# Two-layer attention and expert kernel: the last stage's order of work on five engines, the key rows' swap, and the last expert chunks

## The reference

```python
x = x + L0_xattn(layernorm(x), ctx, ctx, ...)    # 16 heads, causal
x = x + L0_ffn(layernorm(x), ...)                # shared + 64 experts, top 8
x = x + L1_xattn(layernorm(x), ctx, ctx, ...)
x = x + L1_ffn(layernorm(x), ...)                # ternary weights
# L1_xattn, for each head:
corr = irfft(rfft(Q) * conj(rfft(K)))            # along the 64 rows
corr_mean = corr.mean(axis=-1)                   # over the head's 8 columns
top_w, top_idx = top_k(corr_mean, 4)             # the "delays"
top_w = softmax(top_w)
out = sum_i(top_w[i] * roll(V, top_idx[i]))
out = out @ Wo + bo
```

## The kernel before

| lag | what | engine before |
|---|---|---|
| 0 | normed input `held` (L1210, `norm_in`) | GpSimd |
| 1 | transform `l_pf` (L1560), copied to `l_xf` (L1498, L1499) | PE, ACT |
| 2 | `l_pq` = query, key and value rows of each of the two tiles (L1548 to L1551), copied to `l_qkv` (L1493), product `l_pp` (L1352) | PE, ACT, POOL |
| 3 | sums over head columns, `l_sums` (L1437) | DVE |
| 9 | values times weights, `l_rr` in two halves (L1315) | half POOL, half DVE |
| 10 | `l_po` (L1537), `l_oT` (L1486), `l_py` (L1571, L1572) | PE, ACT, PE |
| 11 | added to `x_res` (L1412), statistics (L1428, L1445), `l_rstd` (L1344, L1346) | DVE, POOL |
| 12 to 14 | `l_zn` (L1452), turned `l_pt` (L1584), `xnT` (L1508), `amax` (L1458) | DVE, PE, ACT, DVE |

## Time and profile before

### The profile page before, as it was taken

How to read it: one execution, slowest core, us unless ns; L and a number is a source line. 1 busy time by engine, 2 the same in 40 slices (tenths; PEclk the granted TensorE clock), 3 DMA queues, 4 the chain that set the end, 5 groups by cost and what they waited for, 6 DMA issues and landing times. The chain is left out here.

```text
span 1321.7 us, 30877 instructions
## 1 busy us (share of the span) xinstructions
PE 1262.8 (96%) x9258; PEld 1016.0 (77%) x9258; DVE 1061.2 (80%) x2054; ACT 905.8 (69%) x1472; POOL 821.4 (62%) x868
## 2 busy tenths in 40 slices
PE   6999999996999999999999999999999998899986
PEld 4777777775788887887878887888878886799975
DVE  4878888884987988988977987988977985367786
ACT  3778888883777777777777776777667775566640
POOL 3766666652565665755665665755665666799960
PEclk8999999996999999999999999999999999999998
DMA  4410101001987676777687687677687583110004
GB/s 119 113 30 28 32 28 32 28 16 39 207 193 177 162 181 164 178 189 172 156 191 173 153 191 164 172 185 175 159 194 171 154 194 74 33 29 28 18 2 128
DMA packets 126227, 159.64 MB, mean 121 GB/s; under 512 B 20856, under 2 KB 59520, under 8 KB 126144
## 3 DMA queue, kind: packets, MB, share of 16 engines
q1 hardware_dynamic: 125054, 158.29, 49.7%
q10 hardware_dynamic: 1090, 0.43, 0.1%
HBM read 152.25 MB, written 6.42 MB: 120 GB/s over the span
## 5 line engine op out<-in xcount | busy, mean ns | idle before, releaser
L1032 DVE TENSOR_TENSOR e_m<-e_pu,raw 128x1024 f32<-128x1024 f32 x256 | 309.8, 1212 | 87.5 <-ACT e_pu L1089 55.8
L1089 ACT ACTIVATE e_pu<-e_pu 128x1024 f32<-128x1024 f32 x256 | 258.7, 1010 | 148.7 <-PE e_pu L1125 146.3
L1099 ACT CAST e_mh<-e_m 128x1024 fp32r<-128x1024 f32 x256 | 268.3, 1048 | 60.4 <-DVE e_m L1032 59.1
L1037 DVE TENSOR_TENSOR e_ml<-e_m,e_mh 128x1024 fp32r<-128x1024 f32 x176 | 239.4, 1360 | 20.4 <-ACT e_mh L1099 19.4
L951 POOL TENSOR_TENSOR e_ml<-e_m,e_mh 128x1024 fp32r<-128x1024 f32 x80 | 193.2, 2418 | 90.0 <-ACT e_mh L1099 90.0
L1123 PE MATMUL e_pu<-r_xh,wuh 128*128 128x512 f32 x528 | 215.4, 408 | 2.5 <-PEq L208 1.9
L1134 PE MATMUL e_py<-e_mh,wdh 128*128 128x512 f32 x528 | 208.5, 395 | 3.4 <-ACT held L1076 3.4
L1125 PE MATMUL e_pu<-r_xl,wuh 128*128 128x512 f32 x528 | 209.5, 397 | 0.0
L1124 PE MATMUL e_pu<-r_xh,wul 128*128 128x512 f32 x528 | 209.5, 397 | 0.0
L1135 PE MATMUL e_py<-e_mh,wdl 128*128 128x512 f32 x528 | 209.1, 396 | 0.0
L1138 PE MATMUL e_py<-e_ml,wdh 128*128 128x512 f32 x528 | 168.4, 397 | 2.2 <-POOL e_ml L951 1.4
(11 more groups left out here) (232 smaller groups left out, 2499.6 us busy)
## 6 DMA issues: line engine op xcount, KB each, us to landing
raw<-gates_scratch SPq DMA_DIRECT2D x512, 256.0 KB, 4.3
x_res<-in_x_dram SPq DMA_DIRECT2D x64, 64.0 KB, 1.8
xcT<-in_ctxT_dram SPq DMA_DIRECT2D x64, 64.0 KB, 1.9
held<-in_ctx_dram SPq DMA_DIRECT2D x32, 128.0 KB, 2.1
out_dram<-t_res SPq DMA_DIRECT2D x16, 256.0 KB, 2.3
gates_scratch<-raw SPq DMA_DIRECT2D x17, 128.0 KB, 2.3
raw<-in_L_ffn_W_up_dram SPq DMA_DIRECT2D x4, 512.0 KB, 4.5
raw<-in_L_ffn_W_down_dram SPq DMA_DIRECT2D x4, 512.0 KB, 5.5
```

Of the source, the lines that this page charges most:

```text
L1032: nc.vector.tensor_tensor(flat(m[r % 3][:]), flat(pu[r % 3][:]), flat(gt[i % SPREAD]), ALU.mult).then_inc(gated, 1)
L1037: nc.vector.tensor_tensor(flat(ml[k][:]), flat(m[k][:]), flat(mh[k][:]).bitcast(F32), ALU.subtract).then_inc(m_low[0], 1)
L1089: nc.scalar.activation(flat(pu[k][:]), flat(pu[k][:]), ACT.Silu).then_inc(silued, 1)
L1099: nc.scalar.copy(flat(mh[k][:]), flat(m[k][:])).then_inc(m_high, 1)
```

## The change

In **experts**, `drive` loops over four iterations (chunks 1 to 12) and writes chunks 13 to 15 out, so that work for chunks that don't exist can be left out (`exists`). The padding and its memset go. `norm_in` moves from GpSimd to VectorE.

In **tail**, TensorE begins a step with `l_py` of the item whose `l_oT` was made a step earlier (lag 11 instead of 10), then `l_pf`, `l_po`, `l_pt`, and the two `l_pq` last; in group steps L1578 comes before the two `l_pq` and L1590 between them. L1548's product of the shifted copy is gone, and so is the copy L1499; `l_pq` has three parts instead of four, and ScalarE writes the swapped key rows with two copies of 64 partitions each. `norm_in` runs on VectorE instead of GpSimd, both halves of `l_rr` on GpSimd instead of one, and the order of VectorE's step changes. There are 46 steps.

```diff
 # experts: drive
+    looped = (chunks - 4) // 3 * 3
-            with eng.Fori(0, (chunks - 1) // 3) as g:
+            with eng.Fori(0, looped // 3) as g:
...
-            for n in range(turns, turns + RING):
-                step(n, GROUPS + n % GROUPS, lambda lag, n=n: (n - lag) // GROUPS)
+            for n in range((1 + looped) * GROUPS, turns + RING):
+                step(n, n % (3 * GROUPS), lambda lag, n=n: (n - lag) // GROUPS)
+        def exists(c):
+            return not isinstance(c, int) or c < chunks
 # each step: routing of chunk c + 1 under "if exists(c + 1)", norm of c + 2 under "if exists(c + 2)"
-                    if i == 12:
+                    if i == 12 and exists(c + 2):
                         norm(c + 2)
...
 # GpSimd, end of experts
-                for n in range(2):
-                    entry.norm_in(x_res, y_mean, y_rstd, n)
 # VectorE, end of experts
+                dve.wait_ge(y_rooted, 4)
+                for n in range(2):
+                    entry.norm_in(x_res, y_mean, y_rstd, n)
 # tail: ScalarE's copies of the projections
-                            nc.scalar.copy(qkv[:, n % SLOTS, j], pq[j][:]).then_inc(q_out, 1)
+                            nc.scalar.copy(qkv[:, n % SLOTS, j, 1:4, :], pq[j][:])
+                            nc.scalar.copy(qkv[S:, n % SLOTS, j, 0, :], pq[j][0:S, 1, :])
+                            nc.scalar.copy(qkv[0:S, n % SLOTS, j, 0, :], pq[j][S:, 1, :]).then_inc(q_out, 1)
...
-                        nc.scalar.copy(xf[:, n % 2, :, :, 0:P], pf[n % 2][:])
-                        nc.scalar.copy(xf[:, n % 2, :, 1, P:], pf[n % 2][:, :, 1, 0:S]).then_inc(f_out, 1)
+                        nc.scalar.copy(xf[:, n % 2], pf[n % 2][:]).then_inc(f_out, 1)
 # tail: TensorE's projections
-                            nc.tensor.matmul(pq[j][:, 0, :], k_swapped, cst["w1T"][:, 1, :], start=True, stop=False)
-                            nc.tensor.matmul(pq[j][:, 1, :], q, cst["w1T"][:, 0, :], start=False, stop=False)
-                            nc.tensor.matmul(pq[j][:, 2:4, :], k, cst["w1T"][:, 1:3, :], start=False, stop=False)
+                            nc.tensor.matmul(pq[j][:, 0, :], xf[:, n % 2, j, 0, :], cst["w1T"][:, 0, :], start=True, stop=False)
+                            nc.tensor.matmul(pq[j][:, 1:3, :], xf[:, n % 2, j, 1, :], cst["w1T"][:, 1:3, :], start=False, stop=False)
 # tail: GpSimd
-                        gated(nc.gpsimd, n, 0).then_inc(mixed[0], 1)
-                    if on(s, 0) and s >= 2:
...
-                        entry.norm_in(x_res, y_mean, y_rstd, n)
+                        gated(n, 0)
+                        gated(n, 1).then_inc(mixed, 1)
```

More of the change, by code:

```diff
@@ L955, in step @@
                     c, first = chunk(0), isinstance(n, int) and n < GROUPS
[L956 to L969, removed]
-                    if i == 12:
+                    if exists(c + 1):
+                        if i == 1:
+                            routing.low_part(pool, c + 1, (r // GROUPS + 1) % 3)
+                        if i == 2:
+                            routing.ends(pool, nc.gpsimd, "pool", c + 1)
+                        if i == 3:
+                            routing.fourth_powers(pool, nc.gpsimd, "pool", c + 1)
+                        if i == 4:
+                            routing.denominator(pool, nc.gpsimd, "pool", c + 1)
+                        if i == 9:
+                            routing.weights(pool, nc.gpsimd, "pool", c + 1)
+                        if i == 11:
+                            routing.gates_of(pool, nc.gpsimd, "pool", c + 1)
+                    if i == 9 and not first:
+                        y_root(c - 1)
+                    if i == 12 and exists(c + 2):
                         norm(c + 2)
                 drive(pool, step)
-                for n in range(2):
-                    entry.norm_in(x_res, y_mean, y_rstd, n)
             @block.sync
@@ L1041, in step @@
                     c, first = chunk(0), isinstance(n, int) and n < GROUPS
[L1042 to L1048, removed]
-                            y_add(c - 1)
-                    if i == 6:
-                        routing.compare(dve, c + 1)
-                        routing.invert(dve, c + 1, 0)
@@ L1222, in tail @@
     N = TILES // 2
-    STEPS = N + 15
+    STEPS = N + 14
     SLOTS = 8
@@ L1260, in tail @@
         pf = [psum(f"l_pf{i}", [P, 2, 2, P]) for i in range(2)]
-        pq = [psum(f"l_pq{i}", [P, 4, D]) for i in range(2)]
+        pq = [psum(f"l_pq{i}", [P, 3, D]) for i in range(2)]
         po = psum("l_po", [P, 2, P])
@@ L1290, in tail @@
         c_out = sem("l_c_out")
-        mixed = [sem(f"l_mixed{i}") for i in range(2)]
+        mixed = sem("l_mixed")
         inverted = sem("l_inverted")
@@ L1408, in _ @@
                         choose(g)
+                    if on(s, 0) and s >= 2:
+                        n = s
+                        if n == N - 2:
+                            dve.wait_ge(y_rooted, 3)
+                        dve.wait_ge(transformed, n - 1)
+                        entry.norm_in(x_res, y_mean, y_rstd, n)
+                    if g is not None:
+                        keep(g)
                     if on(s, 11):
@@ L1431, in _ @@
                         invert_sum(g)
+                        scale(g)
+                    if on(s, 11):
+                        n = s - 11
+                        dve.wait_ge(stats, 2 * n + 1)
+                        for j in range(2):
+                            ins = nc.vector.bn_aggr(mv[:, n % 2, j, :], st[:, n % 2, j, :])
+                        ins.then_inc(stats, 1)
                     if on(s, 3):
@@ L1504, in _ @@
                         nc.scalar.copy(cT[:], pw).then_inc(w_out, 1)
+                    for j in range(2):
+                        if on(s, 2):
+                            n = s - 2
+                            at_least(act, mixed, n - SLOTS + 1)
+                            at_least(act, products, n - SLOTS + 1)
+                            act.wait_ge(projected, 2 * n + j + 1)
+                            nc.scalar.copy(qkv[:, n % SLOTS, j, 1:4, :], pq[j][:])
+                            nc.scalar.copy(qkv[S:, n % SLOTS, j, 0, :], pq[j][0:S, 1, :])
+                            nc.scalar.copy(qkv[0:S, n % SLOTS, j, 0, :], pq[j][S:, 1, :]).then_inc(q_out, 1)
+                        if g is not None and j == 0:
+                            act.wait_ge(c_transformed, g + 1)
+                            at_least(act, mixed, 4 * (g - 1))
+                            nc.scalar.copy(cf[:, g % 2].rearrange("p i t h -> p i (t h)"), pab).then_inc(c_out, 1)
                     if on(s, 13):
```

191 lines of the change are left out of this document (84 added, 107 removed).

## The result

Seven runs of the changed kernel gave a median of 1316.3 us (1311.0 to 1318.1), against 1321.1 of the kernel before (1319.1 to 1326.2, seven runs as well). The medians differ by 4.8 us. The ratio estimated from all the runs is 0.9949, with a 95% interval of 0.9935 to 0.9963, which is 6.7 us (4.9 to 8.6). Either way the kernel is a little faster, by about half or less of the 14 us that were forecast. The profiled execution took 1318.1 us, the longest of the seven; its span is 1316.3 (before: 1321.7).

The account below looks back on a forecast made before the run. Experts bound by TensorE, steady tail by TensorE and GpSimd together, the drain by a chain of engines. -3.7 - 1.8 - 8.0 - 1.7 + 1.5 = -13.7 from the median 1321.1 gives 1307; range 1296 to 1318.

Parts of the forecast that it names:

- Experts and the end of the block: Experts lose work for missing chunks, a wait for `e_ml` and one loop jump, -3.7; norms leave GpSimd before tail, -1.8.
- First steps: Steps 2 to 8 of tail: ScalarE's copy of `l_pf` is hidden, a step takes 2.45 us instead of 3.98; -8.0.
- what was given back (1.3): First group of tail: TensorE reaches L1578 1.6 us sooner and waits 0.6 for the fourth `l_sums`; 1.3 off the gain.
- Steady steps: Tail, steps 9 to 34: less TensorE work, nearly all given back waiting for VectorE's chain at L1578; four steps 19.4, -1.7.
- 2.0 between the two: TensorE's wait in a steady group step, taken between 1.4 without collisions and 2.5 us with both.
- the exclusive lock: Rival: VectorE's norms and `l_zn` and GpSimd shut each other out in tail, 4.9 us a step; 1338 us, chance 0.07.
- Drain: Tail from step 34 on: GpSimd's step of 2.5 us is the longest list of the last four steps; +1.5.
- a sign of being wrong: First steps set by ScalarE or VectorE, TensorE waits for `l_rr` or norms, or a group step without a wait.
- The collisions add up: Rival: VectorE's norms fall under `l_pp` in every tail step, TensorE waits 4.0 us a group; 1318 us, chance 0.17.
- The chain is in time: Rival: VectorE gets ahead of the collisions, TensorE waits 0.5 us a group or less in tail; 1298 us, chance 0.20.

Follow-up runs that it names:

- the kernel with the filled wait: Changed kernel with 40 bf16 products that nobody reads made by TensorE ahead of the turn of the weights in each group step: 1314.0 us, ratio 0.9934.
- the kernel with the late turn: Changed kernel with TensorE's turn and transform of the weights one step later, ScalarE's two copies following: 1299.1 us, ratio 0.9832.
- the chain in one piece: Changed kernel with VectorE making keep, add_up, invert_sum and scale directly behind choose, ahead of norms, addition and statistics: 1314.2 us, ratio 0.9937.
- the swap back on TensorE: Changed kernel with one more TensorE product for each `l_pq` and ScalarE copying 512 columns at once: 1317.1 us, ratio 0.9967.

## Why the prediction was wrong

**Experts and the end of the block** (-3.7 and -1.8): -7.2 against -5.5. From the first turned rows of the experts (L726, now L725, at 297.49 and 298.32 us) to the start of tail it is 816.2 us before and 809.0 after. Three parts make it up.

- 5.3 lie behind the affinities of the last real chunk (1048.45 and 1047.39), where 4.5 were forecast. The wait of 1.43 us for `e_ml` went as a whole and not by 0.9; the other terms came in as said. This part is 59.9 us in every trace with the changed experts.
- 0.7 lie in the 14 chunks ahead of that, where 1.0 was forecast. The price was read too low: from the affinities of one chunk to those of the next it is 48.4 to 48.8 us, and 50.3 to 50.7 across a jump back, so a jump costs TensorE 1.6 us or more and not the 1.0 of its longest wait. Leaving the loop cost nothing, as taken (48.72 us across it). But one jump of the kernel before cost only 0.6.
- 1.2 lie ahead of that, where nothing of the sum acts. This part varies by 1.6 us between traces with the same experts, so it is luck.

In the other traces with the changed experts the whole stretch took from 1.9 us less to 0.6 more.

**First steps** (-8.0): -5.8, counted by steps as the prediction did (26.9 against 32.7 us). The 64-partition copies take 0.26 us, as taken, and a step takes 2.43. Too small was what was given back (1.3): TensorE waits 3.4 us at the first turn, 0.9 for `l_sums` and 0.6 for a norm. Behind the first turn the clock fell too, which cost 1.5 us (the same steps take 25.4 us in the kernel with the filled wait). And some 0.9 of the gain belong to the shorter wait at the block's end, as the kernel with the experts' change alone shows.

**Steady steps** (-1.7): +6.1, and this is the step that failed. From step 9 to step 34 there were 119.2 us before (1146.31 to 1265.47) and 125.3 after (1134.17 to 1259.47). The work was right: four steps without the wait are 17.6 us (17.4 forecast). The mechanism and the place of the wait were right too. Its size was "2.0 between the two", and it was 2.6, above the upper bound of 2.5. In the group step that TensorE begins at 1208.15 the chain ran so:

| us into the group step | forecast | measured |
|---|---|---|
| `mark` ends | 1.4 | 2.1 |
| `scale` ends | 3.9 (5.0 with both collisions) | 5.3 |
| TensorE stands at the turn | 2.55 | 2.7 |

The two collisions that the bound took in, `choose` under `l_pp` and `scale` under `l_rr`, cost 0.65 and 0.2 us, less than the 1.1 put for them. What the bound had left out is `l_zn` under `l_rr`: it holds up top, shift and mark by 0.65 us. The prediction let `l_zn` wait for `l_rstd`, but let it run undisturbed; only the rival of the exclusive lock counted it among what collides. It is the change itself that brings this on. In the kernel before, all 42 instructions of `l_zn` from 1150 to 1262 us ran beside GpSimd's norms or its small `l_ve` and `l_rstd`, and took 0.31 to 0.34 us each; now GpSimd's `l_rr` pair stands there, and they take 0.65 to 0.67. That `l_zn` makes the difference is read from the timeline; no run shows it by itself.

By work and wait four steps are 20.2 instead of 19.4, and 0.8 in each of six groups makes 5. The other 2.8 are the clock, which no term of the sum had: it fell twice between steps 9 and 34, and the kernel with the filled wait takes 122.5 us there. A wait of TensorE was priced at its length. The sum also has a slip: 19.4 against 19.56 is -1.0 over six groups, and where the other 0.7 of the -1.7 come from is not said.

**Drain** (+1.5): +1.3, but not for the reason given. GpSimd's list was to be 2.5 us and the longest of the last four steps. It is 2.2, and the last four `l_po` follow each other in 2.17 us instead of 2.39. The price of 0.77 for half of `l_rr` was a mean of 0.63 undisturbed and 0.81 to 0.89 beside VectorE's half. The loss lies ahead of them: TensorE waits 1.0 us for `l_sums` and 1.6 at the last turn (0.6 before), and the granted clock is 0.83 from 1260 to 1270 where it was 1.00. The size is luck.

Of what was named as a sign of being wrong, the changed trace has one wait for a norm (0.6 us) and two for `l_rr` (0.7 together), all at the edges of tail.

**The rivals.** "The collisions add up" gave 1318 with waits of 4.0 (six times 2.0 above 1307 is 1319); the time is near, the wait is not. "The chain is in time" has the time of the kernel with the late turn, 1298 against 1299, though there TensorE comes later and the chain is no faster. The exclusive lock was put at 4.9 us a step, and steady steps without a turn in them are 4.10: that sum does not hold. The Trainium skill (SBUF — State Buffer, Who interferes with whom) is right on the single instruction, by this trace, where GpSimd's is `l_rr` or `l_pp`: `tensor_scalar` and two-input `tensor_tensor` of VectorE end behind it (1.24, 0.94, 1.69 us where 0.60, 0.29, 0.60 are undisturbed). GpSimd's loss, which the prediction found in no row, is in the trace before:

```profile
1262.43 0.43 DVE L1315 TENSOR_TENSOR l_rr<-l_qkv,l_cf 128x256 f32<-128x256 f32 x1 [1.16 <-ACT l_cf L1514]
1262.48 0.87 POOL L1315 TENSOR_TENSOR l_rr<-l_qkv,l_cf 128x256 f32<-128x256 f32 x1 [0.43 <-ACT l_cf L1514]
```

VectorE's half began 0.05 us ahead, and GpSimd's took 0.87 us where 0.63 is undisturbed. The same section of the Trainium skill has a `tensor_tensor` with both inputs in SBUF contend with GpSimd's reads. For GpSimd's `tensor_scalar` this trace does not agree: under the norms of the kernel before, VectorE's `l_rr` took 0.41 or 0.42 us, as it did alone. As long as VectorE has idle time to lose, such collisions cost only where they lie on the chain that TensorE waits for; in the late-turn kernel VectorE has none, and the same collisions are what is left.

What stays open: what of the collisions could be had back. Both kernels with `l_rr` moved closed a ring instead, and one with VectorE's order changed moved the collision to `scale`.

## What to carry to other kernels

Work taken from an engine ahead of a wait is mostly not gained but waited: ask first for the instruction at which the engine will wait next, and whether it can stand later in the order, since here one step of lag was worth 17 us, and of 14 us of TensorE's work taken away ahead of the wait none showed in the time. In a kernel that keeps TensorE at its upper clock, price a long wait at more than its length: here the clock took another 4.5 us in one execution, and about half of that by the medians. A chain that crosses two engines can be held up by any operation in it, so ask of each what the other engine runs beside it, those ahead of the chain's first named operation too. In a pipeline of written-out orders follow each engine's queue once around before moving an instruction: data that are seven steps old do not help if the instruction stands behind one that waits for the newest.

## What the runs showed that I had not expected

- The granted clock fell behind some waits of TensorE, for some 3 us each, about 1.5 us lost: in the changed kernel behind the first turn (a wait of 3.4 us) and behind waits of 2.3 and 2.6 in steady tail, and in the one with the chain in one piece behind waits of 2.1. Behind three others of 2.6 us it did not fall. In the traces with the swap back on TensorE (waits of about 1.5 us in steady tail) and with the filled wait it stayed at 1.00 there. The length of the wait alone does not decide: with the experts' change alone it fell behind a wait of 1.3 us, behind which it had not fallen in the kernel before. What decides stays open.
- The most time was lost to order alone: 58 us by moving two GpSimd instructions of 0.63 us behind one of 1.27.
- VectorE's `l_zn` and `choose` under GpSimd's `l_rr` and `l_pp` end shortly behind them (0.08 and 0.16 us), whatever their own length; under GpSimd's small `l_rstd`, `choose` took its undisturbed 0.29. The addition with one operand in PSUM (L1425) took 0.40 to 0.43 us wherever it stood.
